# Batch 0's scores in two pairs of PSUM banks, values stored 17 columns apart in four buffers, and moved slots in a fused attention and expert kernel

## The reference, cut to what matters

```python
h = _L0_tok_ref(x, L0_tok_embeddings)                 # (8, 256, 256)
h = h + _L0_attn_ref(_layernorm(h), w_qkv, w_proj)    # q, k rotated; softmax(q k^T * hd**-0.5) v; @ w_proj
h = h + _L0_ffn_ref(_layernorm(h), gate_w, expert_w)

def _L0_ffn_ref(x, gate_w, expert_w):
    chosen = argmax(einsum('bsh,eh->bse', x, gate_w))
    return x + einsum('bsef,bse->bsf', einsum('bsh,efh->bsef', x, expert_w), one_hot(chosen))
```

## Time and profile before

| | before |
|---|---|
| median of 3 runs | 310.89 us (310.54 to 310.95) |
| profiled execution, its time | 310.0 us |
| profiled execution, its span | 308.2 us |
| TensorE matmul busy | 283.4 us, 92% |
| VectorE busy | 243.4 us, 79% |
| ScalarE busy | 132.7 us, 43% |
| GpSimd busy | 85.9 us, 28% |
| mean granted clock of TensorE | 0.983 |

### The profile page before, as it was taken

The page is one execution under the profiler, slowest core; times in us unless marked ns, Lnnn a source line. Parts: engine busy times, 40 slices in busy tenths (PEclk is TensorE's granted clock), DMA queues, the critical chain, the costliest instruction groups (busy, mean ns, idle before and its releaser), DMA issues.

```text
span 308.2 us, 5639 instructions
## 1 busy us (share of the span) xinstructions
PE 283.4 (92%) x2063; PEld 203.1 (66%) x2063; DVE 243.4 (79%) x602; ACT 132.7 (43%) x271; POOL 85.9 (28%) x103
## 2 busy tenths in 40 slices
PE   2998799888879999999999999999999999999895
PEld 2775566656646776777767776777666666667674
DVE  8798569968987799887988698878898874656765
ACT  3166117748664534364426433453453444331000
POOL 5736305636265012431222033201200210210300
PEclk9999579999999999999999999999999999999999
DMA  4530410830930580039101940166010010000011
GB/s 117 182 149 17 160 45 6 167 49 14 161 47 5 95 120 2 0 93 147 17 2 36 147 60 2 36 116 94 2 37 1 4 36 2 1 12 26 0 36 34
DMA packets 10803, 17.55 MB, mean 57 GB/s; under 512 B 2024, under 2 KB 4883, under 8 KB 10648
## 3 DMA queue, kind: packets, MB, share of 16 engines
q1 hardware_dynamic: 9988, 16.62, 26.2%
q0 software_dynamic: 768, 0.55, 0.7%
q10 hardware_dynamic: 20, 0.02, 0.0%
HBM read 5.30 MB, written 2.10 MB: 24 GB/s over the span
## 4 chain that ended last, share of the span: by engine, by line
PE 64%; DVE 24%; ACT 5%; issue 3%; DMA 1%; POOL 0%; SPq 0%; DVEq 0%; ACTq 0%
PE e_bank L475 18%; PE f_bank L475 10%; PE o_bank L652 9%; DVE neg_max L1003 7%; PE t_pair L617 5%; DVE acc L1101 4%; PE s_pair L475 4%; PE s_pair L578 3%; PE m_bank L475 3%; PE s_pair L481 2%; PE o_bank L475 2%; PE m_bank L666 2%; PE m_bank L698 2%; ACT probs L867 2%; ACT parts L816 1%
## 5 line engine op out<-in xcount | busy, mean ns | idle before, releaser
L867 ACT ACTIVATE probs<-t_pair 128x512 f32<-128x512 f32 x128 | 69.5, 595 | 80.1 <-PE t_pair L617 79.6
L1003 DVE TENSOR_REDUCE neg_max<-s_pair 128x2 f32<-128x512 f32 x128 | 81.9, 682 | 13.0 <-PE s_pair L578 12.8
L578 PE MATMUL s_pair<-stacks 48*128 48x256 f32 x256 | 49.5, 316 | 1.5 <-DVE neg_max L1003 0.8
L617 PEld LDWEIGHTS t_pair<-stacks 50*128 50x128 f32 x256 | 32.8, 186 | 22.7 <-issue 20.8
L617 PE MATMUL t_pair<-stacks 50*128 50x256 f32 x256 | 46.6, 308 | 1.1 <-DVE neg_max L1003 0.6
L475 PE MATMUL e_bank<-ew_h,y_h 128*128 128x512 f32 x92 | 40.3, 438 | 1.9 <-DVE acc L1101 1.5
L1101 DVE SCALAR_TENSOR_TENSOR acc<-e_bank,mask,acc 128x256 f32<-128x256 f32 x66 | 28.8, 478 | 11.8 <-PE e_bank L475 11.7
L578 PEld LDWEIGHTS s_pair<-stacks 48*128 48x128 f32 x256 | 34.3, 190 | 4.5 <-DVE neg_max L1003 3.5
L475 PE MATMUL e_bank<-ew_l,y_h 128*128 128x512 f32 x92 | 36.4, 396 | 0.0
L394 POOL TENSOR_TENSOR qk<-rope_a,rope_b 128x512 f32<-128x512 f32 x16 | 20.8, 1301 | 56.2 <-DVE rope_b L990 56.2
L475 PE MATMUL e_bank<-ew_h,y_l 128*128 128x512 f32 x92 | 36.2, 394 | 0.0
(11 more groups left out here) (177 smaller groups left out, 542.5 us busy)
## 6 DMA issues: line engine op xcount, KB each, us to landing
stacks<-parts SPq DMA_DIRECT2D x36, 256.0 KB, 6.7
ew_raw<-in_expert_w SPq DMA_DIRECT2D x1, 2048.0 KB, 8.5
out<-res SPq DMA_DIRECT2D x7, 256.0 KB, 2.1
stacks<-parts SPq DMA_DIRECT2D x12, 128.0 KB, 2.8
probs<-in_w_qkv SPq DMA_DIRECT2D x2, 384.0 KB, 3.8
stacks<-max_rows SPq DMA_DIRECT2D x30, 8.0 KB
h<-in_emb,ids POOLq DMA_INDIRECT x16, 2.7
probs<-in_w_proj SPq DMA_DIRECT2D x1, 256.0 KB, 2.7
```

What stands on the lines that cost most here:

```text
L578: m = mm(s_pair[:, half, t * N:(t + 1) * N], stacks[b % STACKS][r:r + KS, pair, 0, t * P:(t + 1) * P], stacks[b % STACKS][r:r + KS, pair, ...
L617: m = mm(t_pair[:, half, c * N:(c + 1) * N], stacks[b % STACKS][r:r + KM, pair, 1, c * P:(c + 1) * P], stacks[b % STACKS][r:r + KM, pair, ...
L867: nc.scalar.activation(probs[:, (2 * v + half) % RING, :, :].rearrange("p c n -> p (c n)"), t_pair[:, half, :], ACT.Exp, scale=SCALE).then ...
L1003: v.tensor_reduce(neg_max[:, k // 4, :, 4 * half + k % 4], s_pair[:, half, :].rearrange("p (t n) -> p t n", t=NT), AX.X, ALU.max, negate=T ...
```

## The change

- `scores_pair`: scores of batch 0 go to `s_pair` for even visits and to `t_pair` for odd ones. A visit then waits for the reductions of the visit before the last. Step 0's first transposed scores wait until all 16 reductions of batch 0 are done. The first maxima are transposed in `e_bank`.
- `vals` becomes a view on a flat buffer in which heads are 17 columns apart (16 values and a one); `outputs` reads 32 columns from there, so the last 15 are the next head's values. The zeros are written only behind the last head. There are four buffers instead of three; `filled` counts eight memsets.
- v of batch 4 moves from slot 5 of step 2 to slot 12 of step 1 (`FOUR`), in `e_bank`, with buffer 0 as its target.
- Opening: the order of TensorE's pieces, of VectorE's and of ScalarE's changes, five fills are added, the second half of `project_qk(2, 1)` moves from step 0 into it, and xn of batch 2 is computed by GpSimd (`normed`) rather than VectorE, ahead of `gather(3)`.
- Step 0: `TWO` puts rotate0 and rotate1 in slots 1 and 3 (from 0 and 1), their transposes in 3 and 5 (from 2 and 4), qk_low in 4 and 6 (from 3 and 5). One fill less in slot 2.
- `POST`: out_project from 8 to 9, gate from 14 to 15, its transpose from 15 to 16 and choose from 15 to 17; 16 and 17 are slots 0 and 1 of the next step. `choose` stands ahead of `select` in VectorE's slot now. `LAST`, the table of batch 7, stays.
- `maxima_slot` is 11 for all batches.

```diff
@@ -17,9 +17,10 @@
 STRIP = 32
+COLS = 17
 N_EXP = 8
 STACKS = 3
-VALS = 3
+VALS = 4
@@ -91,7 +92,8 @@
         unit = sb("unit", [P, HD])
-        vals = [sb(f"vals{i}", [P, NT, NH, STRIP]) for i in range(VALS)]
+        vals_flat = [sb(f"vals{i}", [P, NT * NH * COLS + STRIP - COLS]) for i in range(VALS)]
+        vals = [f[:, 0:NT * NH * COLS].rearrange("p (t h c) -> p t h c", t=NT, h=NH) for f in vals_flat]
         neg_max = sb("neg_max", [P, 2, NT, 8])
@@ -174,10 +176,10 @@
         EARLY = dict(stats=-12, norm=-9, x=-7, x_low=-6, qk0=-5, qk1=-4, rotate0=-3, rotate1=-2, t0=0, low0=1, t1=2, low1=3, v=5)
-        TWO = dict(rotate0=0, rotate1=1, t0=2, low0=3, t1=4, low1=5, v=7)
-        FOUR = dict(FRONT, stats=-10, norm=-8, x=-7, x_low=-6, qk0=-5, rotate0=-3, qk1=-2)
-        POST = dict(o0=2, o1=4, norm0=3, norm1=5, on=6, o_low=7, proj=8, residual=9, stats=10, g_norm=11,
-                    y=12, y_low=13, gate=14, gate_t=15, choose=15)
+        TWO = dict(rotate0=1, rotate1=3, t0=3, low0=4, t1=5, low1=6, v=7)
+        FOUR = dict(FRONT, stats=-10, norm=-8, x=-7, x_low=-6, qk0=-5, rotate0=-3, qk1=-2, v=-4)
+        POST = dict(o0=2, o1=4, norm0=3, norm1=5, on=6, o_low=7, proj=9, residual=9, stats=10, g_norm=11,
+                    y=12, y_low=13, gate=15, gate_t=16, choose=17)
         LAST = dict(o0=2, o1=2, norm0=3, norm1=3, on=4, o_low=5, proj=6, residual=7, stats=7, g_norm=8,
@@ -213,7 +215,7 @@
         def v_bank(k):
-            return o_bank if k < 2 else f_bank
+            return o_bank if k < 2 else e_bank if k == 4 else f_bank
@@ -235,7 +237,11 @@
-            return 10 if b < 3 else 11
+            return 11
+
+        def scores_pair(b, v):
+
+            return t_pair if b == 0 and v % 2 else s_pair
@@ -380,6 +386,12 @@
                 g.tensor_tensor(f_rs[:, :], f_ve[:, :], neg_half[:, :], ALU.pow).then_inc(f_rstd, 1)
+
+            def normed(b):
+                pool.wait_ge(f_rstd, b + 1)
+                for t in range(NT):
+                    g.tensor_scalar(xn[:, t, :], h0[:, b * NT + t, :], f_mv[:, t, 0:1], f_rs[:, t:t + 1],
+                                    ALU.subtract, ALU.mult).then_inc(f_normed, 1)
@@ -457,6 +469,7 @@
             f_rs_of(2)
+            normed(2)
             gather(3)
@@ -484,7 +497,7 @@
                 elif b >= 3:
-                    wait(pe, v_ok, b)
+                    wait(pe, v_ok, 4 if b == 5 else b)
                     wait(pe, qkl_ok, (b - 1) * NT)
@@ -496,6 +509,9 @@
                     pass
+                elif b == 4:
+                    wait(pe, xl_ok, b + 1)
+                    wait(pe, on_ok, NT)
                 elif b >= 2:
@@ -519,7 +535,7 @@
                 elif b == 2:
-                    wait(pe, qkl_ok, 2)
+                    wait(pe, mt_ok, 1)
                 elif b == 3:
@@ -571,21 +587,26 @@
                     wait(pe, stack_in, (b - 2) * 96 + 96)
-                wait(pe, max_ok, b * NH + 2 * v - half)
+                if b == 0 and v == 1:
+                    pe.wait_ge(roped, 2 * 2 * NT)
+                if b == 0:
+                    wait(pe, max_ok, 2 * v - 2 - half if v > 1 else 0)
+                else:
+                    wait(pe, max_ok, b * NH + 2 * v - half)
...
                 r, pair = place(2 * v + half)
-                m = mm(s_pair[:, half, t * N:(t + 1) * N], stacks[b % STACKS][r:r + KS, pair, 0, t * P:(t + 1) * P],
+                m = mm(scores_pair(b, v)[:, half, t * N:(t + 1) * N], stacks[b % STACKS][r:r + KS, pair, 0, t * P:(t + 1) * P],
                        stacks[b % STACKS][r:r + KS, pair, 1, :], start=True, stop=True)
...
-                pe.wait_ge(roped, 2 * 2 * NT)
+                pe.wait_ge(qkl_ok, NT)
                 pe.wait_ge(ml_ok, 1)
                 for t in range(NT):
-                    m = tr(t_bank[1][0:16, N + t * P:N + (t + 1) * P].bitcast(F32R),
+                    m = tr(e_bank[0:16, N + t * P:N + (t + 1) * P].bitcast(F32R),
                            max_parts[:, 0, t, :, :, :].rearrange("p i a j -> p (i a j)"), ident_r[:, :])
@@ -607,9 +628,11 @@
                     pe.wait_ge(roped, 2 * 2 * NT)
-                    pe.wait_ge(filled, VALS + 1)
+                    pe.wait_ge(filled, 2 * VALS + 1)
                 if v % 4 == 0:
                     wait(pe, m_in[v // 4], b * 32 + 32)
+                if v == 0 and b == 0:
+                    pe.wait_ge(max_ok, NH)
                 wait(pe, exp_ok, b * NH + 2 * v + half - 1)
@@ -649,7 +672,8 @@
                     for j in range(4):
-                        m = mm(o_bank[STRIP * j:STRIP * (j + 1), 0:N], vals[b % VALS][:, c, head(4 * g + j), :],
+                        at = (c * NH + head(4 * g + j)) * COLS
+                        m = mm(o_bank[STRIP * j:STRIP * (j + 1), 0:N], vals_flat[b % VALS][:, at:at + STRIP],
                                probs[:, (4 * g + j) % RING, c, :], start=(c == 0), stop=(c == NT - 1),
@@ -712,6 +736,7 @@
                     pe.wait_ge(ew_l_ok, 8)
+                    pe.wait_ge(v_ok, 5)
                 if b == NB - 3 and n == 1:
@@ -726,11 +751,8 @@
                         visit(b, s // 2)
-                        if b == 0 and s == 0:
-                            project_qk(2, 1, [1])
-                            pe.wait_ge(xl_ok, 3)
                         if b == 0:
-                            fill(m_bank, 3 if s == 0 else 4 if s == 2 else 1)
+                            fill(m_bank, 3 if s < 4 else 1)
                     if here(b, 0) and s == 3:
@@ -790,23 +812,28 @@
             qk_transpose(1, 0)
+            project_v(0, [0])
             visit(-1, 1)
             qk_transpose(1, 1)
+            project_v(0, [1])
             visit(-1, 2)
+            fill(m_bank, 1)
+            project_v(1, [0])
+            visit(-1, 3)
             x_transpose(2)
-            visit(-1, 3)
-            project_v(0, [0])
+            project_v(1, [1])
+            visit(-1, 4)
             first_max_transpose()
-            visit(-1, 4)
-            project_v(0, [1])
             project_qk(2, 0, [0])
             visit(-1, 5)
-            project_v(1, [0])
             project_qk(2, 0, [1])
+            fill(m_bank, 1)
             visit(-1, 6)
-            project_v(1, [1])
+            project_qk(2, 1, [0])
+            fill(m_bank, 1)
             visit(-1, 7)
-            project_qk(2, 1, [0])
+            project_qk(2, 1, [1])
+            fill(m_bank, 2)
             steps(step)
@@ -850,7 +877,7 @@
                 wait(act, mt_ps, b * 2 + u + 1)
-                turned = t_bank[1] if b == 0 and u == 0 else o_bank
+                turned = e_bank if b == 0 and u == 0 else o_bank
                 copy(max_rows[:, u, :], turned[0:16, N:2 * N]).then_inc(mt_ok, 1)
@@ -938,12 +965,12 @@
             qk_high(1, 1)
+            values(0)
             qk_high_again(1, 0)
...
             x_high(2)
+            values(1)
             max_row(0, 0)
-            values(0)
-            values(1)
             steps(step)
@@ -1001,7 +1028,7 @@
                     v.tensor_reduce(neg_max[:, k // 4, :, 4 * half + k % 4],
-                                    s_pair[:, half, :].rearrange("p (t n) -> p t n", t=NT), AX.X, ALU.max,
+                                    scores_pair(b, k)[:, half, :].rearrange("p (t n) -> p t n", t=NT), AX.X, ALU.max,
                                     negate=True).then_inc(max_ok, 1)
@@ -1134,6 +1161,8 @@
                         g_norm_b(k)
+                    for k in batches(post, "choose", g_at):
+                        choose(k, k % 2)
                     if here(b, -2) and s > 0 and unit_in(b, s - 1) is not None:
@@ -1159,9 +1188,6 @@
                         y_low(k, k % 2)
-                    for k in batches(post, "choose", g_at):
-                        choose(k, k % 2)
-
             dve.sem_inc(acc_ok, 1)
@@ -1177,8 +1203,6 @@
             x_low(0)
-            for i in range(VALS):
-                v.memset(vals[i][:, :, :, HD:STRIP], 0.0).then_inc(h_zero, 1)
             f_norm_b(1)
@@ -1189,16 +1213,15 @@
             rotate(1, 1)
-            dve.wait_ge(h_zero, NB + VALS)
             for i in range(VALS):
                 v.memset(vals[i][:, :, :, HD:HD + 1], 1.0).then_inc(filled, 1)
+                v.memset(vals_flat[i][:, NT * NH * COLS:], 0.0).then_inc(filled, 1)
             maximum(0, 0)
             f_norm_a(2)
+            qk_low(1, 0)
             maximum(0, 1)
-            f_norm_b(2)
-            qk_low(1, 0)
+            qk_low(1, 1)
             maximum(0, 2)
-            qk_low(1, 1)
             maximum(0, 3)
```

## The result

The changed kernel takes 318.07 us (median of 4 runs, 317.0 to 319.18), the kernel before 310.72 (310.23 to 310.95), a ratio of 1.0239 with a 95% interval of 1.0193 to 1.0285. The sign was forecast, the size was not: +7.35 us against +3.45, and 318.07 lies 0.5 us above the range's end. The profiled run has a time of 319.18 and a span of 317.4, 9.2 over the span before; it is the longest of the four, so the spans lie farther apart than the medians. The runs of the changed kernel fall in two pairs, 2 us apart, with a mean granted clock of 0.978 and 0.982 in the longer ones and 0.989 in the shorter.

What follows compares the result with a forecast made beforehand. TensorE was taken as busiest, nearly full in middle steps but not in the opening. Opening -6.3, step 0 +4.6, step 1 +1.4, step 2 -1.9, late projection and gate the rest: +3.45, 314.3 us; own range 312.4 to 316.0.

Steps and rivals of the forecast that it cites:

- The opening: Before step 0: scores in two pairs of banks and the new order start step 0 at 39.8, not 46.1: -6.3 us.
- (c): Rival: the clock falls in the opening after all, 3.3 us more, 317.6 us; chance 0.12.
- Step 0: Later rotations and GpSimd's late sum hold TensorE: +2.1 us by order, +2.5 by the clock.
- Rival (a): The clock holds in step 0, so its 2.5 us go away: 311.8 us; chance 0.18.
- Step 1: v of batch 4 moved in and visit 6 starting 1.06 later, two stalls covered: +1.4 us together.
- Part 4: POST's moves: late projection +0.85 in each of steps 2-4, +0.95 in 5 and 6, +0.6 in 7; gate +0.6 at step 8.
- Rival (b): VectorE's slack absorbs the delay of residual, 4.45 us less: 309.8 us, with rival (a) 307.4; chance 0.19.
- v and the gate: v of batch 4: 1.43 us into step 1, out of step 2; choose takes 0.45 more from step 2, gate +0.6 at step 8.
- The values 17 apart: Loads for outputs from values stored 17 columns apart cost the same as before: 0.
- Rival (d): Loads from the values stored 17 apart get slower, 4.0 us over 512 loads: 318.3 us; chance 0.04.
- The sum: All terms over the whole kernel: +3.45 us, span 308.2 to 311.65, median time 314.3 us.

Runs made afterwards that it cites:

- e7: The kernel before with only out_project moved from slot 8 to slot 9: 320.15 us, ratio 1.0317.
- e3: The changed kernel with out_project back at the end of slot 8: 309.16 us, ratio 0.9964.
- e2: The changed kernel with 13 fills in slot 5 of step 0, ahead of the transposes that wait for GpSimd: 315.97 us, ratio 1.0189.
- e1: The changed kernel with GpSimd's two gathers and first low part of expert weights in step 0 moved from slot 1 to 4: 315.36 us, ratio 1.0181.
- e4: The changed kernel with six fills in slot 9 of step 1, ahead of x_transpose(4): 316.54 us, ratio 1.0206.
- e8: The kernel before with only gate, its transpose and choose moved as in the change: 309.81 us, ratio 0.998.
- e9: The changed kernel with out_project in slot 8, TWO as before and v of batch 4 back in step 2: 303.76 us, ratio 0.9794.
- e11: e9 with values 32 columns apart again, zeroed by VectorE, in three buffers: 305.31 us, ratio 0.9831.
- e10: The changed kernel with 13 fills in slot 5 of step 0 and six in slot 9 of step 1: 314.68 us, ratio 1.0148.
- e5: The changed kernel with out_project back in slot 8 and the slots of TWO as before: 303.39 us, ratio 0.9779.
- e6: e5 with gate, its transpose and choose back in their old slots: 304.32 us, ratio 0.9808.

## Why the prediction was off

The step that failed is the price of the late projection. The prediction gave it 0.85 to 0.95 us in each middle step, 0.6 in step 7 and 1.06 in step 1, 6.1 in all, and the clock behind its new wait nothing; the order alone measured 7.8 (e7), and with the clock of step 1 taking the projection back was worth 8.5 to 8.9 (e3). Smaller misses in the same direction are the opening, `TWO` in step 2 and the gate in step 6.

**The opening: right, 0.6 short.** The walk gave visits 2, 3 and 4 at 30.0, 31.5 and 33.2 and visits 5, 6 and 7 at 35.2, 36.6 and 38.1; they start at 29.60, 31.25, 32.98, 35.14, 36.71 and 38.28. The last reduction ends at 40.1, not 39.8. The clock held, as I had taken it to, so (c) is out. xn on GpSimd took 2.44 us (28.90 to 31.34), not at most 1.29; it was hidden, with less room than I had thought.

**Step 0: right in size.** I said 2.1 for the order and 2.5 for the clock; e2 splits it 2.25 and 1.76. The mechanism, a sum behind two gathers and a low part, is what e1 shows. My 3.5 us of idle time were 3.26. The clock's term came out near for another reason than mine: I took 5 us of dense work at 1.2 GHz, and the clock was low for some 7 us, of which TensorE worked for 4 and stood in the wait for the rest. Rival (a), that the clock holds, is refuted.

**Step 1: the clock left out.** I worked out that the projection would be held back by x_transpose and its xn, and that the delay would cost about 1.06 at visit 6. The wait is there, 1.39 us at 80.40. What I left out is the clock behind it. I had priced the clock for step 0, where the waits were long, and had written nothing for step 1, where the same change made one of 1.4 us in a stretch that already had a wait of 1.2. I took the stalls of 0.66 and 0.70 us as removed and did not ask whether the ones in their place are longer. Of the +4.87, e4 gives 3.0 to the clock; the rest, 1.9, stands beside my 1.4. That 1.4 does not follow from its own terms: 1.43 for v and 1.06 at visit 6, less the 0.70 ahead of the gate, are 1.79, and 1.13 if the 0.66 goes off as well. The runs bear out the first: v +1.24, projection +1.33, gate -0.73, together 1.84. And the fall is not certain at this wait: in e7's profiled run the clock held behind the same 1.39 us, so I could have priced it only with a chance.

**Part 4, the projection: the right mechanism, sized too small.** e7 prices the order alone at 7.8 us, where my own terms for it come to 5.05 plus what I had put into step 1. The terms were short by 0.27 in step 1, 0.18 in each of steps 2 to 4, 0.25 in each of steps 5 and 6 and 0.23 from step 7 on. In step 4 of e7, h starts 20.49 into the step, before it was 19.48: 1.01 later and not 0.85, and the step is 1.03 longer. In after, steps 5 and 6 cost 1.26 and 1.54, not 0.95; the projection makes 1.19 and 1.21 of that (e7), and in step 6 the moved gate adds 0.35 (e8), which after shows as a new wait of 0.35 ahead of an expert, for a select that now stands behind choose; I had put 0 there. In step 7 y_transpose waits 1.26, where I had put 0.6, and at the start of step 8 the gate's transpose waits 0.46; before, TensorE waited for neither:

```profile
233.16 0.50 PE L488 MATMUL e_bank<-ew_h,y_h 128*128 128x512 f32 x1 [0.35 <-DVE acc L1124]
...
277.37 0.66 PE L714 MATMUL m_bank<-ident,yn 128*128 128x128 f32 x4 [1.26 <-DVE yn L1070]
...
283.57 0.29 PE L730 MATMUL m_bank<-ident,gate_rows 16*128 16x16 f32 x2 [0.46 <-ACT gate_rows L843]
```

Rival (b), that VectorE has slack for the delay, is refuted by every middle step.

**v and the gate: right as a sum, wrong in part.** v's move is +1.24 and -1.49, where I had 1.43 and 1.45 (e9), and the gate's is neutral (e8). Step 2 gained 0.56 and not 1.05, since `TWO` costs 0.52 there; I had priced it in step 0 alone and called the later restack hidden.

**The values 17 apart: right.** The group of loads has 109 ns in e9 and in e11, and 109 before; after's 111 come with its low clock. The Trainium skill (SBUF — State Buffer, section "Door 1: The DMA port swizzle") says that each access that crosses to a new 16-byte line costs something. The trace shows no such cost for these loads of 32 columns that start at multiples of 68 bytes, 109 ns either way; the measurement decides. Rival (d) is out.

**The sum.** By span I was 5.75 us low: 0.6 in the opening, -0.6 in step 0, 3.5 in step 1 (3.0 of it the clock), 0.5 in step 2, and 1.75 from step 3 on. Of that the clock makes 2.3 (1.76 and 3.0 against 2.5) and the order 3.5. In the medians the clock has a smaller part, as two of the four runs of after lost less to it: without the clock my sum was +0.95, and the two runs of e10 at the full clock are 3.5 to 4.1 over their kernel before, about 3 more; the clock makes the last 1. The clock's term of step 0, 0.7 too high, hid a part of this by luck; nearly all the other errors went one way. The range missed too, as its bounds took one cause at a time: the clock was bounded in the opening and in step 0, not in a further place, and the terms of part 4 had no upper bound, although an error in them counts in six steps.

## What to carry to other kernels

A piece that is moved later by one slot in every step costs its delay times the number of steps once its reader is on the chain: price that first, since here 1 us of a swap came to 8.5 us of a 310 us kernel, and the opening's gain was lost with it. Wherever a change makes TensorE idle near other idles, price its clock there too, in each such place. And ahead of moving a small piece on a helper engine, list what stands in that engine's queue: two gathers and a low part (3.6 us) turned the later rotations into a wait of 3.26 us; the waits of step 0 cost 2.75 us and the clock 1.76.

## What the runs showed of the hardware

- The granted clock fell to 0.50 behind idles of 1.01 and 0.67 us (e1) and behind one of 1.39 (after, e1, e2), and held behind 1.39 us in the profiled run of e7. Behind 1.21 us it fell in after and e10, and held in before, in e1 to e5 and in e7. In the opening of before it fell where the last idles of TensorE had been 0.37, 0.33 and 0.48 us. No length of a single idle stretch separates these cases.
- A fall costs some 1.5 to 1.8 us (1.76 in step 0; 1.5 for each of the two in step 1), and runs of one kernel differ by about that, with a mean clock 0.005 to 0.01 apart: 317.0 and 319.18 in after, 303.24 and 305.4 in e6, 313.74 and 315.94 in e10. The low stretch in step 0 of after lasts about 7 us, one in step 1 about 3.5; it cost hardly more, as 2.7 us of it lie in a wait.
- Matmuls that nobody reads, put into a wait, kept the clock at 1.00 in step 0 of e2 at no price of their own: the second transposes started 9.58 us into the step with thirteen of them and 9.52 without.
- At the very start of the kernel the clock's column does not tell the pace: it reads 1.00 from 8.0 to 11.5 us of before, where the matmuls of 512 columns start 0.43 us apart, against 0.24 from 12.06 on.
- A gather holds GpSimd's queue for 1.0 to 1.16 us, and between two of them lies 0.3; a sum queued behind two gathers and a low part started at 48.56 in after, and at 46.07 in e1 without them.
- The two instructions of 128x256 that make xn of batch 2 took GpSimd 2.44 us in after and VectorE 0.78 in before.
